# A four-stage transformer block: setup, norms and the attention's opening in one interleaved stage, and a middle stage with full-height operands

## The reference

```python
x = x + tanh(g_xattn[0]) * L0_xattn(ctx, layernorm(x), mask, ...)   # latent attention
x = x + tanh(g_ffn[0])   * L0_ffn(layernorm(x), ...)                # 8 experts, best 2
x = x + tanh(g_xattn[1]) * L1_xattn(layernorm(x), ctx, ...)         # 16 heads of 16
x = x + tanh(g_ffn[1])   * L1_ffn(layernorm(x), ...)                # quantised gate, up, down

def L0_xattn(c, lat, mask, ...):          # 16 heads of 64, lat has 2048 rows
    xn, ln_lat = layer_norm(c, g1, b1), layer_norm(lat, g2, b2)
    q = ln_lat @ Wq
    k, v = split(concatenate([xn, ln_lat]) @ Wkv)
    w = softmax(where(mask, (q * scale) @ (k * scale).T, -max))
    return (w @ v) @ Wout

def L0_ffn(x, ...):
    # softmax over x @ router_w + router_b, best two of eight, gelu(x @ W1 + b1) @ W2 + b2

def L1_xattn(x, c, ...):
    q, k, v = x @ Wq.T + bq, c @ Wk.T + bk, c @ Wv.T + bv
    return softmax(q @ k.T * scale) @ v @ Wo.T + bo
```

## Time and profile before

| | |
|---|---|
| median of 3 runs | 3393.74 us (3390.88 to 3395.65) |
| profiled execution, its time | 3392.96 us |
| profiled execution, its span | 3391.1 us |
| mean granted TensorE clock | 0.956 of full |
| PE busy | 3001.4 us (89%), 21696 instructions |
| DVE busy | 2453.9 us (72%), 3029 |
| ACT busy | 1817.4 us (54%), 2033 |
| POOL busy | 2082.1 us (61%), 968 |

### The profile page before, as it was taken

How to read it: one execution, slowest core, us unless ns; L and a number is a source line. 1 busy time by engine, 2 the same in 40 slices (tenths; PEclk the granted TensorE clock), 3 DMA queues, 4 the chain that set the end, 5 groups by cost and what they waited for, 6 DMA issues and landing times. The chain is left out here.

```text
span 3391.1 us, 53618 instructions
## 1 busy us (share of the span) xinstructions
PE 3001.4 (89%) x21696; PEld 1101.4 (32%) x21704; DVE 2453.9 (72%) x3029; ACT 1817.4 (54%) x2033; POOL 2082.1 (61%) x968
## 2 busy tenths in 40 slices
PE   3589999999999999999999999998697799999947
PEld 1223333333333333333333333322354133333324
DVE  5567777778767877778777876782535888888758
ACT  3155445555555545544555555544443588888833
POOL 0077898888888889879888888989510111111022
PEclk9699999999999999999999999999698799999969
DMA  1000000000000000000000000000210100000000
GB/s 59 5 1 1 1 7 1 1 1 7 1 1 7 1 1 7 1 1 7 1 1 1 2 1 1 1 1 1 74 23 13 42 7 6 7 8 6 4 0 26
DMA packets 24536, 28.72 MB, mean 8 GB/s; under 512 B 6431, under 2 KB 21216, under 8 KB 24290
## 3 DMA queue, kind: packets, MB, share of 16 engines
q1 hardware_dynamic: 24290, 25.30, 2.6%
...
...
## 5 line engine op out<-in xcount | busy, mean ns | idle before, releaser
L413 POOL TENSOR_TENSOR a_acc_p<-a_acc_p,a_prob 128x1024 f32<-128x1024 f32 x704 | 1726.1, 2452 | 299.5 <-ACT a_prob L483 217.8
L543 DVE TENSOR_REDUCE a_part_max<-wide 128x2 f32<-128x1024 f32 x896 | 1088.4, 1215 | 475.6 <-PE wide L713 474.9
L483 ACT ACTIVATE a_prob<-slot,a_mask_bias 128x1024 f32<-128x1024 f32 x928 | 987.6, 1113 | 732.1 <-PE slot L738 712.7
L753 PE MATMUL bank<-a_prob,a_val 128*64 128x512 f32 x3712 | 898.8, 606 | 2.1 <-ACT a_prob L483 2.1
L713 PE MATMUL wide<-a_k_hi,a_q_hi 64*128 64x512 f16 (+1 forms) x2048 | 365.9, 369 | 147.4 <-DVE a_part_max L543 134.9
L1025 ACT ACTIVATE a_prob<-slot,a_mask_bias 128x1024 f32<-128x1024 f32 x416 | 455.4, 1116 | 65.5 <-PE slot L1183 52.2
L1067 DVE TENSOR_REDUCE a_part_max<-wide 128x1 f32<-128x512 f32 x514 | 332.7, 681 | 37.3 <-PE wide L1171 20.4
L753 PEld LDWEIGHTS bank<-a_prob,a_val 128*64 128x64 f32 x3712 | 226.6, 136 | 394.9 <-issue 290.2
L738 PE MATMUL slot<-a_q_hi,a_k_lo 64*128 64x512 f16 x1856 | 353.1, 377 | 0.0
L738 PE MATMUL slot<-a_q_hi,a_k_step_hi 64*128 64x512 f16 x1728 | 328.7, 377 | 2.6 <-ACT a_prob L483 2.5
L738 PE MATMUL slot<-a_q_lo,a_k_step_hi 64*128 64x512 f16 x1728 | 328.3, 377 | 0.0
...
## 6 DMA issues: line engine op xcount, KB each, us to landing
...
x_res<-in_x SPq DMA_DIRECT2D x1, 2048.0 KB, 9.1
a_q_op<-a_hi SPq DMA_DIRECT2D x128, 16.0 KB, 1.8
...
```

The costliest lines, as they stand in the source:

```text
L413: nc.gpsimd.tensor_tensor(acc, before, prob[:, k % R, :], ALU.add).then_inc(added_p, 1)
L483: nc.scalar.activation(prob[:, k % R, :], m.slot[k % 2][:, :], ACT.Exp, bias=mbias[:, t:t + 1]).then_inc(probs_ready, 1)
L543: nc.vector.reduce_max(part_max[:, w % 2, :, j, c], pairs, AX.X).then_inc(max_used, 1)
L753: ins = nc.tensor.matmul(av[r, :], val[g % 2][:, t, r], prob[:, k % R, h * QB:(h + 1) * QB], start=(t == 0), stop=(t == NT - 1), tile_posi ...
```

## The change

**Opening.** Setup, both norms and the latent stage become one block. x and the context are loaded in blocks of 512 rows, and the order of each engine runs over these blocks. The remainders of the normalised rows go from DVE to POOL, the high part of the first group's weights from POOL to ACT. Masked rows are now filled with the first key before they are split: the normalised context is multiplied by the mask, and `fill_ctx` adds what POOL has put into `fill`. The first group's steps and their remainders (L522, L533 before) go from DVE to POOL. Pairs alternate in the lead between `wide` and one half of the score buffers (`slot[1]`), and a pair waits for the maximum before the last. In the first unit they run over the query blocks of one key chunk before the next chunk, and the 20 jobs of the first group are laid between pairs (`job_after_pair`, `open_jobs`). The main loop's order is kept, but the split of group 1's weights falls to its very beginning.

**Middle stage.** The operands of two and of eight rows get 128, with zeroes. The keys' biases too are now added by such matmuls, `kv_y` goes, and the keys' remainder goes from POOL to DVE (`k_low`). The jobs' order changes from group by group to keys of group 0, values of all, keys of groups 1 to 3. On ACT the splitting of the expert weights comes later.

```diff
+        def pair_bank(n):
+            return pairs_slot if n < a.lead and n % 2 else pairs_wide
+
+        def pair_of(w, i):
+
+            return divmod(i, a.blocks)[::-1] if w == 0 else divmod(i, a.full)
...
+            sp.dma_start(gates[:, :], gates_in[0:1, :].broadcast_to([P, 4])).then_inc(gates_loaded, 16)
+            for b in range(NL // 4):
+                src = x_in[b * QB:(b + 1) * QB, :].rearrange("(t p) d -> p t d", p=P)
+                sp.dma_start(m.x[:, 4 * b:4 * b + 4, :], src).then_inc(x_loaded[b], 16)
...
+            pool.wait_ge(affine_loaded, 32)
+            pool.wait_ge(wscale_set, 1)
+            pool.wait_ge(w_first, 1)
+            nc.gpsimd.tensor_tensor(w_lo[:, :], w_st[:, :], w_hi[:, :], ALU.subtract).then_inc(w_split, 1)
+            for n in range(6):
+                row_low(n)
+            pool.wait_ge(mask_loaded, 32)
+            pool.wait_ge(affine_edge, DC)
+            for c in range(DC):
+                nc.gpsimd.tensor_scalar(fill[c], valid_u8[:, :], to_first[:, c:c + 1], first_key[:, c:c + 1],
+                                        ALU.mult, ALU.add).then_inc(affine_edge, 1)
+            row_low(6)
+            row_low(7)
+            for b in range(a.nk - a.nx):
+                row_low(8 + 2 * b)
+                row_low(9 + 2 * b)
+                step(b)
+                if b:
+                    step_low(b - 1)
+            for n in range(a.nx, a.nk):
+                step(n)
+                step_low(n - 1)
+            step_low(a.nk - 1)
...
+            measure_x(0)
+            measure_x(1)
+            aggregate(0, 8)
+            measure_x(2)
+            first_norm(0)
+            measure_x(3)
+            second_norm(0)
+            norm_x(0)
+            aggregate(8, 8)
+            norm_x(1)
+            first_norm(1)
+            measure_ctx(0)
+            second_norm(1)
+            norm_x(2)
+            norm_x(3)
+            for b in range(1, len(ctx_loaded)):
+                measure_ctx(b)
+            aggregate(NL, NCT)
...
-            dve.wait_ge(masks_ready, 1)
-            parts = [(x, ct, c) for x, ct in ((m.xh, m.ch), (m.xl, m.cl)) for c in range(DC)]
-            for x, ct, c in parts:
-                nc.vector.tensor_tensor(ct[:, c, :], ct[:, c, :], valid[:, :], ALU.mult).then_inc(zeroed_rows, 1)
-            for n, (x, ct, c) in enumerate(parts):
-                dve.wait_ge(zeroed_rows, n + 1)
-                nc.vector.scalar_tensor_tensor(ct[:, c, :], hidden[:, :], x[:, c, 0:1], ct[:, c, :], ALU.mult, ALU.add).then_inc(replaced, 1)
...
+            for b in range(len(ctx_loaded)):
+                norm_ctx(b)
+            project(0, a.nx)
             for n in range(a.lead):
+                if n % 4 == 0 and n // 4 < len(ctx_loaded):
+                    fill_ctx(n // 4)
                 pair(n)
+                if n in a.query_low_after:
+                    project(0, a.query_low_after[n])
                 if n == NT - 1:
                     max_of(0)
-            shift_of(0)
+                if n == NT + 1:
+                    shift_of(0)
...
-                if i == 0 and u == 0:
+                if i == 0 and u == 0 and g:
                     pe.wait_ge(hi_done, kq(g, a.nkq - 1))
-                if n:
+                if w == 0:
+                    c = pair_of(0, i)[1]
+                    key = c if c < a.nx else c + NU
+                    pe.wait_ge(hi_done, max(kq(0, key), kq(0, a.nx)))
+                elif w == 1 and i == 0:
+                    pe.wait_ge(hi_done, kq(0, a.nx + 1))
+                elif w == 2 and i == 0:
+                    pe.wait_ge(hi_done, kq(0, a.nx + NU - 1))
+                if n >= a.lead:
                     pe.wait_ge(max_used, n)
-                blocks = [i // a.full] if i < NT - 1 else range(a.blocks)
+                elif n >= 2:
+                    pe.wait_ge(max_used, n - 1)
+                pairs = pair_bank(n)
+                blocks = [pair_of(w, i)[0]] if i < NT - 1 else range(a.blocks)
...
+        nc = len(self.chunks)
+        kinds = [("k", 0)] + [("v", g) for g in range(self.groups)] + [("k", g) for g in range(1, self.groups)]
+        self.jobs = [(g, kind, c) for kind, g in kinds for c in range(nc)]
+        self.nj, self.routing, self.turning = len(self.jobs), 3 * nc, nc
...
+            dve.wait_ge(bias_chain, 3)
+            link(nc.vector.tensor_scalar(bias[:, :, :], bias[:, :, :], WSCALE, None, ALU.mult))
+            link(nc.vector.tensor_copy(bias_hi[:, :, :], bias[:, :, :]))
+            nc.vector.scalar_tensor_tensor(bias_op[0:2, :, :], bias_hi[:, :, :], m.ident[0:2, 1:2], bias[:, :, :], ALU.mult, ALU.subtract).then_inc(bias_ready, 1)
             x_low(0, 1)
             scale(0, 3)
             x_low(0, 2)
+            k_low(0)
...
-            link(nc.vector.tensor_scalar(bias[:, :], bias[:, :], WSCALE, None, ALU.mult))
-            link(nc.vector.tensor_copy(bias_hi[:, :], bias[:, :]))
-            nc.vector.scalar_tensor_tensor(bias_op[:, :], bias_hi[:, :], m.ident[0:2, 1:2], bias[:, :], ALU.mult, ALU.subtract).then_inc(bias_ready, 1)
+            for p in range(1, NC):
+                k_low(p)
...
+                pe.wait_ge(bias_ready, 1)
                 out = jbank(p)
-                passes = [(keep.w_hi, m.ch), (keep.w_hi, m.cl), (keep.w_lo, m.ch)]
+                passes = [(kv_hi, m.ch), (kv_hi, m.cl), (kv_lo, m.ch)]
+                own_bias = bias_op[:, 0 if kind == "k" else 1, g * P:(g + 1) * P]
                 if kind == "k":
                     for q, (wt_, x) in enumerate(passes):
                         for d in range(DC):
-                            col = (DC + d) * P
-                            ins = nc.tensor.matmul(out[:, 0:w], wt_[:, g, col:col + P], x[:, d, at:at + w],
-                                                   start=(q == 0 and d == 0), stop=(q == 2 and d == DC - 1))
+                            nc.tensor.matmul(out[:, 0:w], wt_[:, g, d * P:(d + 1) * P], x[:, d, at:at + w], start=(q == 0 and d == 0), stop=False)
+                    ins = nc.tensor.matmul(out[:, 0:w], own_bias, ones[:, 0:w], start=False, stop=True)
                 else:
-                    pe.wait_ge(bias_ready, 1)
                     for b in range(w // P):
                         own = out[:, b * P:(b + 1) * P]
-                        nc.tensor.matmul(own, ones[:, :], bias_op[:, g * P:(g + 1) * P], start=True, stop=False)
                         for q, (wt_, x) in enumerate(passes):
                             for d in range(DC):
-                                col = (2 * DC + d) * P
-                                ins = nc.tensor.matmul(own, x[:, d, at + b * P:at + (b + 1) * P], wt_[:, g, col:col + P],
-                                                       start=False, stop=(q == 2 and d == DC - 1))
+                                nc.tensor.matmul(own, x[:, d, at + b * P:at + (b + 1) * P], wt_[:, g, (DC + d) * P:(DC + d + 1) * P],
+                                                 start=(q == 0 and d == 0), stop=False)
+                        ins = nc.tensor.matmul(own, ones[:, 0:P], own_bias, start=False, stop=True)
```

556 lines of the change are left out of this document (382 added, 174 removed).

## The result

| | before | changed |
|---|---|---|
| median | 3392.31 us (3390.24 to 3395.65, 4 runs) | 3298.01 us (3297.26 to 3298.79, 4 runs) |
| profiled execution, its span | 3391.1 us | 3296.6 us |
| mean granted TensorE clock | 0.956 | 0.968 |

The ratio is 0.9718, with a 95% interval of 0.9703 to 0.9732: 94 us less, where 76 were forecast.

What follows compares the result with a forecast made beforehand. PE bounds the main loop (95% busy); in stage 1 up to 172 us the stages wait for one another. Stage 1 -70.7, loop 0, middle's opening +1, experts -6.4: -76.1, so 3318 us; range 3300 to 3338.

Steps and rivals of the forecast that it cites:

- Stage 1, the lead: First maximum to first scores, 71.8 us before: two buffers remove the .71 idling, DVE's sum 44 to 45 us.
- Rival 1: Lead of stage 1: the clock stays low, PE is last, scores start at 114.8; 12 more, 3330; chance .17.
- rival 4: Lead: the two buffers don't alternate as meant, each pair waits two maxima; 33 x .5 more, 3334; chance .05.
- Stage 1, the front: Start to first maximum, 100.4 us before: fused blocks bring it to 53, or 57.6 with PE at half clock.
- Main loop: First scores to middle stage: same order on all five engines, POOL has 14% to spare, so 0 change.
- Rival 5: Main loop: POOL stays one add behind, every unit waits 2.45; 78 more, 3396, slower than before; chance .03.
- Middle, opening: Middle stage's start to first spread, 86 us before: block savings against added biases and delays, +1, between -3 and +8.
- the delay of key job 0: Middle's opening: key job 0 waits for DVE's three bias operations behind a normalising, starting some 8.5 us later.
- Experts: Middle stage's expert steps: spreads with 128 rows instead of 8 save .20 in each of 32 steps, 6.4 less.
- Rival 2: Middle stage: narrow operands are not what costs, so .20 x 84 is lost; 3335; chance .08.
- Rival 3: Lead: DVE stands behind POOL again and again, ten steps each waiting 1.2; 3330; chance .12.
- The case with everything at its best: Whole kernel: every bound at its best, -76.6 - 3 - 6.4 = -86, 3308; 3302 if the fills cost 1.6.

## Why the prediction was right or wrong

The time came out 20 us under the forecast: 9 in the front, 6 in the middle's opening, and 1 to 2 each in the lead, the main loop and the experts. Without the first two it would have been some 15 us longer and inside the range.

**Stage 1, the lead: right, with two sizes that cancel.** 44.1 us against 44 to 45 at full clock. That the idling ahead of the maxima goes is shown from both sides, by taking the second buffer away and by adding it alone. The sum had 31 maxima at 1.23 ahead of the first scores; there are 33, 1.13 apart, which comes to the same. PE's work was put at 26 us and was 32.9, without effect, since DVE is last. The clock, which the forecast left open, is lower wherever one buffer is used: .52 before and .78 with two buffers there; .97 in the changed kernel and about .8 with one buffer there. Rival 1 (the clock stays low, 3330) fell, and so did rival 4.

**Stage 1, the front: 57.6 forecast, 48.6 measured.** This step failed by the most, and two of its terms were mis-sized. The fills were put in with 3.6 each, "nearest to its fp16 subtraction"; they took 1.7, near the end that the 1.6 of DVE's cast gave: 3.7 us for the two, and the doubled fills show that they count. And 4.6 was added for half clock all through the front (53 became 57.6). The trace has half clock from 15 to 28 and from 40 to 45, and it costs far less, since PE is not last there: .5 behind the last rows of x, by the run with idle matmuls, and ahead of them the profiles differ by 1.1 in all. The chain was right link by link: remainders, fills, normalising, the query's remainder, the bank, keys 2 and 3, fill, maximum. The fourth link of it, a single operation in DVE's list, was worth 4.8 to 5.9 us of the first maximum, and I counted it without asking what it would be to move it.

**Main loop: 1.8 less instead of 0.** Rival 5, one add of POOL more in every unit, did not come: the loop is no slower. The last maxima of the second unit come 56.4 after the first scores instead of 58.0, which is little more than the table load of 1.3 that had been counted. The other 1.5 of this stretch's 3.1 goes along with the clock: the kernel before has two short pieces at half clock late in the loop, the changed one has one. That the edit brought this about is not shown.

**Middle, opening: +1 forecast, -4.8 measured.** This is the second step that failed. The saving of a block was sized right (.21 each). Mis-sized was the delay of key job 0: "some 8.5 later" was 3.1 (22.4 us after the stage's start against 19.3), since the normalising ahead of it was held up less. In the group of that line the longest operation is 1.5 us, where the earlier trace rows has 8.5:

```profile
L1896 DVE TENSOR_SCALAR mid_xn<-x_res,mid_mv,mid_rstd x32: 395/410/1519, 2315.3 to 2507.0; 128x256 f32<-128x256 f32 x32
```

Four of the eight such operations right ahead of it fall into a pause in POOL's new list (2325.2 to 2329.3), the other four get through one beside each POOL operation. And the forecast had no term for a change of the clock: it took the slow one over from before. These are the stretches from key job 0 to the first spread, before and changed:

```profile
2413.40:2480.40 67.00, 63.92 (x601) 40.33 (x602) 25.13 (x80) 43.46 (x76) 46.37 (x40) 0.87 0.19 40
2334.00:2393.10 59.10, 51.73 (x616) 38.09 (x616) 23.80 (x92) 34.37 (x62) 31.28 (x35) 0.96 0.16 34
```

Before, the clock was half from 2427 to 2440, in the middle of it, with PE full; value blocks came .97 apart there. Now it is full from 2339 on. PE's busy time falls by 12.2 us. The blocks less the keys' biases account for 7.6 of it by the forecast's own terms, and some 12 us less at half clock for the rest (they are worth up to 6, an estimate from the two rows' clocks). PE then idles 4.95 ahead of the first spread, so what ends last now is not PE but the laying out of the keys. The prediction named that wait. By these rows a somewhat smaller delay of key job 0 would have brought nothing.

**Experts: 7.8 instead of 6.4.** The .20 per step is exact: 3.04 us instead of 3.24. The rest is the first step, 2.2 us shorter; before, the clock is at half for twice as long in it. The groups of 12 expert-bias matmuls, which got 128 rows as well, add nothing in the three steps where they can be told apart. Rival 2 fell, by two runs.

**Rival 3** (DVE behind POOL again and again) is half true: it happens to normalising, with 3.5, 2.8 and 1.3 us lost in the front, and not to the maxima. A small operation with two SBUF inputs, L854, lasts .68 beside POOL's subtraction in the front, where its like, L787, takes .17.

The 94.5 us are thus 70.7 + 10 (front 9, lead 1), 1.8, 4.8 and 7.8, less .6. The case with everything at its best had been put at 3302. It was passed because three terms lay beyond the bounds given to them: the middle's opening (bound -3), the experts (bound -6.4) and the main loop (0, without a bound). All three go along with the clock in part. The range was also narrower above than the prediction's own worst case, 3338 against 3343.
